# The last stage of a fused audio tower: bias rows without cleared rows, weight rests by another instruction form, and probabilities that travel with the tokens

## The chip, the cores and the metric

The kernel runs on one core of a Trainium2 chip. The metric is the device time of that core in microseconds (us). The median of three runs before the change is 1778.48 us (1774.12 to 1779.3).

## What is computed

The reference is a two-layer tower over 4 batches of 750 tokens of 192 numbers each: a token mixer, a linear-attention block with a causal part, a gated mixture of 8 experts with the best two taken, a window attention with relative positions, and last a mixture of 8 experts with the best one taken. Only the last is changed by intent:

```
xt = _layernorm(h).reshape(-1, 192)            # 3000 tokens
logits = xt @ Ws + bs;  probs = softmax(logits)
routes = argmax(probs);  prob_max = max(probs)
hid = gelu(xt @ W1[route] + b1[route])         # 192 -> 768
y = hid @ W2[route] + b2[route]                # 768 -> 192
out = h + y * prob_max
```

Everything is float32.

## The kernel before, in words

One program holds the four stages one behind the other; the function `moe` (L789 on) is run twice, once gated (name `m0`, the second stage) and once not (name `m1`, the last stage). In `m1`, token row t of a batch lies on partition p, with 125 partitions and 24 tiles, so the whole `h` is a tile of 125 x 24 x 192.

**Front part of the last stage.** The five engines run from instruction lists of their own and wait on semaphores. DVE takes the statistics and normalises (L1314), TensorE turns the tiles (L1068) and makes the logits (L1079), ACT brings them out (L1236, L1241) and takes the exponential (L1260). DVE finds each token's expert (L1394 to L1410), TensorE counts (L1101, L1102), and DVE works out a slot for every token: 31 groups ("tiles") of 128 slots, each with one expert. The list of tokens per slot comes from a product of two one-hot tables (`lane1` L1451, then L1111) and is turned into indices `take` and `give` (L1461 to L1476). `lane1` shares its memory with the normalised tokens, so DVE waits (`s_X`) until these have been stored.

**The rows X.** SP stores h and the normalised tokens side by side in DRAM as a row of 2 x 192 numbers per token (L940). A tensor of 125 partitions is stored in two parts, partitions 0 to 111 and 112 to 124. GpSimd gathers 128 rows by `take` (L1006) when all of X is stored (`s_X`) and `take` is there.

**Weights in two parts.** For accuracy each product is made of three: weights and tokens are split into a rounded value and its rest. ACT makes the rounded weights (`round_weights`, L1225 to L1227, three instructions an expert), DVE the rests (`rest_of_weights`, L1309 and L1310, a subtraction of two tensors each). `w1[:, e, 3, :]` holds the rest of rows 128 to 191 in partitions 0 to 63 and, in partitions 64 and 96, the bias in two parts; GpSimd clears partitions 64 to 127 of it first (L998, eight instructions), and the tokens' side `xB` has ones there. SP puts the two bias rows in place (L957).

**Order before the loop.** ACT rounds experts 0 to 2 between its logits work and 3 to 7 behind the exponential. DVE makes the rests 0 to 2 early, and 3 to 7 behind `take`; then it makes the probabilities (L1481 to L1484), splits them in three bf16 parts and spreads them into a table `tileP` (L1492 to L1496). TensorE waits for all weights, turns the first two gathered groups (L1118, L1119), with ACT (L1272 to L1275) and DVE (L1506, L1507, L1510) splitting them, makes the first group's first products (L1129) and then 24 products of `lane1` and `tileP` (L1138) that put each slot's probability in PSUM, from which DVE adds up `prob` (L1556, L1558).

**The loop.** For each group TensorE turns the next but one group, turns the hidden values (L1176), makes the next group's first products (L1129) and this group's second products (L1190). DVE copies (L1523), adds the bias (L1539) and multiplies by the probability and adds the residual `hres` (L1543), a copy of the gathered h (L1510). GpSimd scatters to the output and gathers the group four further on.

Of the kernel before, what the change touches and what calls it, by code (L numbers as in the profile page):

```python
# [12 lines left out]
F32 = mybir.dt.float32  # L13
# [9 lines left out]
E = len(KS) * D  # L23
# [718 lines left out]
PARTS = 3  # L742

FIRST = ((0, 0), (0, 1), (1, 0), (2, 2), (2, 3))
BHI, BLO = 64, 96
# [6 lines left out]
class Moe:  # L752
# [3 lines left out]
    def __init__(self, name, top, width, gated):  # L756
# [9 lines left out]
        self.wide = E if gated else 2 * E  # L766
# [14 lines left out]
def moe(nc, keep, A, h, ident, cfg, out, st=None, w1=None, wr=None, row=None, room=None, share=None, Y=None,  # L781
# [4 lines left out]
    with ctx:  # L786
# [14 lines left out]
        with ExitStack() as late:  # L801
# [3 lines left out]
            hres = None if cfg.gated else late.enter_context(nc.sbuf_tensor(f"{name}_hres", [SLOT, RING, E], F32))  # L805
# [56 lines left out]
        part = None if cfg.gated else sb("part", [P, PARTS, NT], BF16)  # L862
        prob = None if cfg.gated else sb("prob", [128, S])
# [18 lines left out]

        with ExitStack() as early:
            tileP = None if cfg.gated else early.enter_context(
                nc.sbuf_tensor(f"{name}_tileP", [P, NT, PARTS, S], BF16))
# [33 lines left out]
        s_wb, s_wh, s_wl = (None if cfg.gated else sem(k) for k in ("wb", "wh", "wl"))  # L919
# [4 lines left out]
        s_part, s_prob, s_b2, s_hr = (None if cfg.gated else sem(k) for k in ("part", "prob", "b2", "hr"))  # L924
        stored = 16 * len(ROW_PARTS) * B * (1 if cfg.gated else 2)
# [3 lines left out]
        def _(sp):  # L929
# [21 lines left out]
            if not cfg.gated:  # L951
                sp.dma_start(b2[:].rearrange("p x e -> p (x e)"), A[f"{name}_b2"].partition_broadcast(128)
                             ).then_inc(s_w, 16)
                sp.wait_ge(s_z, 3)
# [11 lines left out]
        def _(pool):  # L966
# [27 lines left out]
            if not cfg.gated:  # L994
                pool.memset(xB[64:128].bitcast(F32), 1.0)
            if not cfg.gated:
                for e in range(NE):
                    last = pool.memset(w1[64:128, e, 3, :].bitcast(F32), 0.0)  # L998
                last.then_inc(s_z, 1)
                pool.wait_ge(s_z, 3)  # L1000
# [56 lines left out]
        def _(pe):  # L1057
# [77 lines left out]
            def probabilities():  # L1135
                pe.wait_ge(s_part, 1)
                for t in range(NT):
                    last = nc.tensor.matmul(psY[:, 256:256 + PARTS * S], lane1[:, 0, t, :],  # L1138
                                            tileP[:, t, :, :].rearrange("p n s -> p (n s)"),
                                            start=(t == 0), stop=(t == NT - 1))  # L1140
                last.then_inc(s_prob, 1)
# [11 lines left out]
            pe.wait_ge(s_xc, 2)  # L1153

# [6 lines left out]
            if not cfg.gated:  # L1161
                probabilities()
# [37 lines left out]
        def _(act):  # L1200
# [102 lines left out]
        def _(dve):  # L1303
# [3 lines left out]
            def rest_of_weights(e):  # L1307
                dve.wait_ge(s_wh, e + 1)
                v.tensor_tensor(w1[:, e, 1, :], w1[:, e, 1, :].bitcast(F32), w1[:, e, 0, :].bitcast(F32), ALU.subtract)  # L1309
                v.tensor_tensor(w1[0:64, e, 3, :], w1[0:64, e, 3, :].bitcast(F32), w1[0:64, e, 2, :].bitcast(F32),  # L1310
                                ALU.subtract).then_inc(s_wl, 1)
# [97 lines left out]
            else:  # L1409
                v.tensor_copy(msk[:], oh[:, 0]).then_inc(s_m, 1)  # L1410

# [69 lines left out]
            link(v.tensor_reduce(lm[:], lg[:], AX.X, ALU.add))  # L1481
            link(v.reciprocal(lm[:], lm[:]))
            for k in range(top):
                link(v.tensor_tensor(pe_[:, k, :], pe_[:, k, :], lm[:], ALU.mult))  # L1484
# [1325 lines left out]
```

## Time and profile before

| | |
|---|---|
| median of three runs | 1778.48 us |
| the profiled execution | 1779.27 us |
| its span | 1777.5 us |
| TensorE matmul busy | 1545.6 us, 87% |
| VectorE (DVE) busy | 1198.3 us, 67% |
| ScalarE (ACT) busy | 990.7 us, 56% |
| GpSimd (POOL) busy | 343.4 us, 19% |
| DMA packets, bytes | 61940, 94.86 MB |

The last stage starts at 1547.5 us of the span and the loop's first product at 1621.3 us. Shares over the whole span are of little use here, since the change touches some 75 us; the stage has to be read in order of time.

### The profile page before, as it was taken

How to read it: one execution, taken by the hardware profiler on the slowest of the kernel's cores; microseconds unless marked ns; L12 is line 12 of the kernel's file. 1: busy time of each engine (PE TensorE's matmuls, PEld its weight loads, DVE VectorE, ACT ScalarE, POOL GpSimd, SP SyncE). 2: the span in 40 equal slices, each digit the busy share in tenths (PEclk: the TensorE clock that was granted, in tenths of full speed). 3: DMA queues.
4: the chain of work that ended last, by engine and by line, in shares of the span. 5: the costliest groups of instructions: out<-in, count | busy, mean ns of one | idle time of the engine just before them, and what ended most of it. 6: DMA issues, size and time to landing. Idle time of an engine off the chain costs nothing. (4 is left out here: it accounts for less than half of the span.)

```text
span 1777.5 us, 32284 instructions
## 1 busy us (share of the span) xinstructions
PE 1545.6 (87%) x10815; PEld 1432.0 (81%) x10816; DVE 1198.3 (67%) x2259; ACT 990.7 (56%) x1818; POOL 343.4 (19%) x507
## 2 busy tenths in 40 slices
PE   4873899945999999899999899899999999646997
PEld 4762899944899899898899899799999889526996
DVE  3878555547785786785787686687777587485553
ACT  6433222224777578577577678577668657262221
POOL 4130566650100110110010010010010000103443
PEclk6886899976998999999899999999999899757999
DMA  8203111145101101100110110110110100191121
GB/s 257 68 23 95 45 56 57 58 118 141 43 11 37 43 11 37 45 11 18 29 43 10 30 44 19 28 43 19 29 43 19 28 8 19 45 311 46 59 61 30
DMA packets 61940, 94.86 MB, mean 53 GB/s; under 512 B 15645, under 2 KB 46512, under 8 KB 61423
## 3 DMA queue, kind: packets, MB, share of 16 engines
q1 hardware_dynamic: 52606, 72.92, 13.9%
q0 software_dynamic: 9200, 20.21, 3.9%
q8 instruction: 78, 1.28, 0.3%
q14 instruction: 56, 0.45, 0.1%
HBM read 72.58 MB, written 21.06 MB: 53 GB/s over the span
## 5 line engine op out<-in xcount | busy, mean ns | idle before, releaser
L2690 DVE TENSOR_TENSOR a_Plo<-a_PT,a_Phi 125x756 fp32r<-125x756 f32 x288 | 281.9, 979 | 72.5 <-ACT a_PT L2415 71.5
L2415 ACT ACTIVATE a_Phi<-a_S 125x756 fp32r<-125x756 f32 x288 | 231.2, 803 | 152.0 <-PE a_O L2209 128.4
L2580 DVE TENSOR_REDUCE a_nmx<-a_M 125x1 f32<-125x752 f32 x248 | 232.7, 938 | 102.9 <-PE a_M L2084 101.9
L1904 POOL TENSOR_TENSOR a_qlo<-a_work,a_qhi 127x750 fp32r<-127x750 f32 x48 | 79.2, 1659 | 1012.6 <-PE a_S L2190 510.9
L2415 ACT ACTIVATE a_PT<-a_S 125x756 f32<-125x756 f32 x288 | 230.3, 800 | 0.0
L1129 PE MATMUL m_psG<-m_w,m_xT 128*128 x788 | 167.3, 351 | 5.1 <-issue 2.3
L2190 PE MATMUL a_S<-a_qhi,a_khi 128*125 128x378 f32 x576 | 153.5, 348 | 10.0 <-DVE a_nmx L2580 6.8
L2202 PE MATMUL a_O<-a_Phi,a_vhi 125*128 125x378 f32 x576 | 150.3, 342 | 1.4 <-issue 1.1
L2209 PE MATMUL a_O<-a_Plo,a_vhi 125*128 125x378 f32 x576 | 147.5, 337 | 0.4 <-DVE a_Plo L2690 0.2
L2190 PE MATMUL a_S<-a_qhi,a_klo 128*125 128x378 f32 x576 | 147.6, 338 | 0.0
L2190 PE MATMUL a_S<-a_qlo,a_khi 128*125 128x378 f32 x576 | 147.0, 336 | 0.0
L2205 PE MATMUL a_O<-a_Phi,a_vlo 125*64 125x378 f32 x576 | 146.4, 336 | 0.0
L1129 PEld LDWEIGHTS m_psG<-m_w,m_xT 128*128 128x128 f32 x788 | 136.6, 191 | 12.1 <-issue 10.4
L1190 PE MATMUL m_psY<-m_w,m_hidT 128*128 x696 | 130.0, 330 | 2.6 <-DVE m_hidT L1523 2.6
L2084 PE MATMUL a_M<-a_khi,a_qhi 127*125 127x376 f32 x496 | 128.4, 340 | 0.4 <-DVE a_nmx L2580 0.4
L1190 PEld LDWEIGHTS m_psY<-m_w,m_hidT 128*128 128x128 f32 x696 | 114.3, 189 | 9.4 <-issue 9.4
L2209 PEld LDWEIGHTS a_O<-a_Plo,a_vhi 125*128 125x128 f32 x576 | 104.1, 189 | 13.9 <-DVE a_Plo L2690 3.7
L2190 PEld LDWEIGHTS a_S<-a_qhi,a_khi 128*125 128x125 f32 x576 | 100.2, 188 | 16.9 <-issue 10.5
L1272 ACT ACTIVATE m_xT<-m_psX 128x128 fp32r<-128x128 f32 x85 | 23.6, 277 | 159.9 <-PE m_psX L1119 83.5
L2202 PEld LDWEIGHTS a_O<-a_Phi,a_vhi 125*128 125x128 f32 x576 | 102.1, 190 | 10.7 <-issue 9.3
L2190 PEld LDWEIGHTS a_S<-a_qhi,a_klo 128*125 128x125 f32 x576 | 104.2, 187 | 0.0
L2190 PEld LDWEIGHTS a_S<-a_qlo,a_khi 128*125 128x125 f32 x576 | 104.0, 187 | 0.0
(431 smaller groups left out, 3017.1 us busy)
## 6 DMA issues: line engine op xcount, KB each, us to landing
a_qhi<-a_rdens SPq DMA_DIRECT2D x48, 187.5 KB, 3.3
m_w<-in_m_w SPq DMA_DIRECT2D x16, 384.0 KB, 7.2
a_wkv<-a_w4k SPq DMA_DIRECT2D x8, 768.0 KB, 4.9
a_wq<-a_w4q SPq DMA_DIRECT2D x8, 768.0 KB, 6.3
a_wkv<-a_w4v SPq DMA_DIRECT2D x8, 768.0 KB, 5.9
m_w<-in_m_w SPq DMA_DIRECT2D x8, 576.0 KB
m_X<-m_xn SPq DMA_DIRECT2D x8, 504.0 KB
m_w<-in_m_w SPq DMA_DIRECT2D x16, 192.0 KB, 7.5
```

The costliest lines, as they stand in the source:

```text
L1129: last = nc.tensor.matmul(psG[buf][:, g, 0:half], tokens, w1[0:rows_, bass.ds(e, 1), k, g * half:(g + 1) * half].rearrange("d o f -> d (o ...
L1190: last = nc.tensor.matmul(psY[:, 0:E], hidT[:, k * 128:(k + 1) * 128], w2[:, bass.ds(here, 1), k, :].rearrange("f o e -> f (o e)"), start= ...
L1272: nc.scalar.activation(xT[:, buf, 0, :], psX[:, 0:SLOT], ACT.Copy)
L1904: pool.tensor_tensor(qlo[0:ONE, u % HG % QLO, :], work[0:ONE, u % HG, 0:L], qhi[0:ONE, u % HG, :].bitcast(F32), ALU.subtract).then_inc(sg[ ...
L2084: last = nc.tensor.matmul(bank[0:P, a, 0:376], qhi[0:ONE, u % HG, c * P:(c + 1) * P], khi[0:ONE, u % HG, a * 374:a * 374 + 376], start=Tru ...
L2190: last = nc.tensor.matmul(psS[wd % 2][0:P, a, 0:HP], kk[:, u % HG, at], qq[:, PART[a]:PART[a] + HP], start=(x == 0), stop=(x == 2))
L2202: nc.tensor.matmul(psO[:, a, 0:HP], vhi[:, c, u % HG, :], Phi[:, wd % 2, at[a]], start=(c == 0), stop=False)
L2205: nc.tensor.matmul(psO[0:HD, a, 0:HP], vlo[:, c, u % HG, :], Phi[:, wd % 2, at[a]], start=False, stop=False)
L2209: last = nc.tensor.matmul(psO[:, a, 0:HP], vhi[:, c, u % HG, :], Plo[:, wd % 2, at[a]], start=False, stop=(c == CH - 1))
L2415: last = nc.scalar.activation(to[:, wd % 2, :].rearrange("p (a l) -> p a l", a=2), psS[wd % 2][0:P, :, 0:HP], ACT.Exp, scale=SCALE)
L2580: v.tensor_reduce(nmx[:, u % 2, c:c + 1], bank[0:P, :, 0:376], AX.XY, ALU.max, negate=True).then_inc(sg["max_ready"], 1)
L2690: v.tensor_tensor(Plo[:, wd % 2, :], PT[:, wd % 2, :], Phi[:, wd % 2, :].bitcast(F32), ALU.subtract).then_inc(sg["exp_rest"], 1)
```

## The change

In the last stage only:

- The rows of X get one number more (385 instead of 384). ACT stores each token's probability behind its row, one DMA with 3000 elements of 4 bytes, each in its own row; `s_X` counts it too. The gathered group then holds its probabilities as column 384, `hres` copies 193 columns, and L1543's successor reads the probability from there. The bf16 parts, `tileP`, the 24 products and the sums in PSUM go.
- DVE makes the probabilities right behind the expert's mask, and the rest of expert 3 behind them, while it waits for the counts; ACT rounds expert 3 before the exponential and experts 4 to 7 behind the store.
- The bias rows lie in partitions 64 and 65, so nothing has to be cleared (the eight GpSimd instructions go), and the product over these rows takes 66 rows instead of 97.
- The rests are written as one instruction with three operands, (w x 1.0) - rounded.
- TensorE turns the first two groups before it waits for the weights (in both `moe` stages), and DVE splits the first group before the rest of expert 7.

```diff
-BHI, BLO = 64, 96
+BHI, BLO = 64, 65
...
-        self.wide = E if gated else 2 * E
+        self.wide = E if gated else 2 * E + 1
...
+        stored = 16 * (len(ROW_PARTS) * B * (1 if cfg.gated else 2) + (not cfg.gated))
...
-                for e in range(NE):
-                    last = pool.memset(w1[64:128, e, 3, :].bitcast(F32), 0.0)
...
-            pe.wait_ge(s_eid, 1)
-            pe.wait_ge(s_w, 16 * (NE + (0 if cfg.gated else 3)))
-            if not cfg.gated:
-                pe.wait_ge(s_wl, NE)
-                pe.wait_ge(s_z, 3)
             for j in range(2):
                 pe.wait_ge(s_in[j], 16)
                 if j:
                     pe.wait_ge(s_xc, 1)
                 to_columns(j)
             pe.wait_ge(s_xc, 2)
+            pe.wait_ge(s_eid, 1)
+            pe.wait_ge(s_w, 16 * (NE + (0 if cfg.gated else 3)))
+            if not cfg.gated:
+                pe.wait_ge(s_wl, NE)
+                pe.wait_ge(s_xo, 1)
...
-            if not cfg.gated:
-                probabilities()
...
+            if not cfg.gated:
+                round_weights(soon)
             act.wait_ge(s_ls, 1)
             nc.scalar.activation(lg[:], lg[:], ACT.Exp).then_inc(s_ex, 1)
...
-                for e in range(soon, NE):
+                act.wait_ge(s_prob, 1)
+                act.dma_start(X[:, 2 * E:].rearrange("(t p) o -> p (t o)", p=P), pe_[:, 0, :],
+                              allow_slow_non_contiguous=True).then_inc(s_X, 16)
+                for e in range(soon + 1, NE):
                     round_weights(e)
...
-                v.tensor_tensor(w1[:, e, 1, :], w1[:, e, 1, :].bitcast(F32), w1[:, e, 0, :].bitcast(F32), ALU.subtract)
+                v.scalar_tensor_tensor(w1[:, e, 1, :], w1[:, e, 1, :].bitcast(F32), 1.0, w1[:, e, 0, :].bitcast(F32),
+                                       ALU.mult, ALU.subtract)
...
                 v.tensor_copy(msk[:], oh[:, 0]).then_inc(s_m, 1)
+                link(v.tensor_reduce(lm[:], lg[:], AX.X, ALU.add))
+                link(v.reciprocal(lm[:], lm[:]))
+                v.tensor_tensor(pe_[:, 0, :], pe_[:, 0, :], lm[:], ALU.mult).then_inc(s_prob, 1)
+                rest_of_weights(3)
...
-                for e in range(3, NE):
+                for e in range(4, NE):
+                    if e == NE - 1:
+                        rest_of_tokens(0, 0)
                     rest_of_weights(e)
+                rest_of_tokens(0, 1)
...
-                        v.scalar_tensor_tensor(y[:, j, :], y[:, j, :], prob[:, bass.ds(RING * i + j, 1)],
-                                               hres[:, j, :], ALU.mult, ALU.add).then_inc(s_y, 1)
+                        v.scalar_tensor_tensor(y[:, j, :], y[:, j, :], hres[:, j, E:], hres[:, j, 0:E], ALU.mult,
+                                               ALU.add).then_inc(s_y, 1)
```

## Rows read from the trace of the kernel before

**Rows 1.** The chain that ended last, last stage: start us, us, what.

```profile
1551.63 4.74 DVE m_xn L1314 x6
1591.18 3.28 DVE m_lane L1451
1598.20 0.86 DVE m_w L1309
...
1611.93 0.45 PE m_psX L1118
...
1614.67 3.56 PE m_psG L1129 x10
1618.24 1.91 PE m_psY L1138 x24
...
1620.60 0.73 PE m_psH L1176 x6
1621.33 1.74 PE m_psG L1129 x10
```

**Rows 2.** Timeline of DVE: start us, us, engine, line, operation, [idle before].

```profile
1558.68 1.83 DVE L1314 TENSOR_SCALAR m_xn<-h,m_mv,m_rstd 125x192 f32<-125x192 f32 x6
1582.87 0.36 DVE L1414 COPY m_tot<-m_psG 128x192 f32<-128x192 f32 x1 [1.74 <-PE m_psG L1102]
1606.80 0.34 DVE L1481 TENSOR_REDUCE m_lm<-m_lg 125x24 f32<-125x192 f32 x1
1607.73 0.18 DVE L1492 CAST m_part<-m_pe 125x24 bf16<-125x24 f32 x1
```

**Rows 3.** Timeline of ACT.

```profile
1576.01 0.28 ACT L1241 ACTIVATE m_lgT<-m_psX 128x125 f32<-128x125 f32 x1 [1.22 <-PE m_psX L1079]
1578.31 0.36 ACT L1260 ACTIVATE m_lg<-m_lg 125x192 f32<-125x192 f32 x1 [2.03 <-DVE m_lg L1387]
1580.10 0.82 ACT L1225 ACTIVATE m_w<-m_w 128x768 fp32r<-128x768 f32 x1
...
1582.54 0.83 ACT L1225 ACTIVATE m_w<-m_w 128x768 fp32r<-128x768 f32 x1
```

**Rows 4.** Timeline of POOL.

```profile
1550.21 6.05 POOL L998 MEMSET m_w<- 64x768 f32 x8
1599.02 1.82 POOL L1006 DMA_INDIRECT m_xg<-m_X,m_take  x1 [40.18 <-DVE m_take L1476]
```

**Rows 5.** DVE groups by shape, whole span: busy us, mean ns | idle before.

```profile
L1539 DVE TENSOR_TENSOR m_y<-m_psY,m_b 128x192 f32<-128x192 f32 x31 | 11.1, 358 | 69.0 <-PE m_psY L1190 55.9 <-issue 13.0
L1396 DVE SCALAR_TENSOR_TENSOR m_tmp<-m_tmp,m_iotx 125x192 f32<-125x192 f32 x3 | 1.1, 357 | 0.1
L1400 DVE TENSOR_TENSOR m_oh<-m_iotx,m_idx 125x192 f32<-125x192 f32 x3 | 1.1, 357 | 0.1
```

**Rows 6.** DMA, 1588 to 1596 us, 40 slices: GB/s.

```profile
GB/s 507 461 392 415 392 392 392 507 479 369 415 369 392 392 484 438 415 415 392 369 392 438 422 522 430 353 422 430 430 399 430 445 307 231 62 31 0 0 46 31
```

**Rows 7.** DMA, 1604 to 1612 us: GB/s by slices of 0.2 us (the gathers).

```profile
GB/s 207 161 92 323 184 15 0 0 0 230 138 292 261 62 0 0 0 92 138 184 361 192 16 0 0 0 0 0 0 0 0 0 0 0 0 0 0 0 0 0
```

**Rows 8.** DMA queues, 1562 to 1563 us: packets, MB, share of 16 engines.

```profile
q1 hardware_dynamic: 90, 0.21, 56.1%
q0 software_dynamic: 90, 0.19, 52.3%
```

**Rows 9.** DMA busy tenths by 0.0125 us, 539.1 to 539.6 us: a store of 150 pieces of 40 bytes from 75 partitions.

```profile
DMA  0000000001333337656465420000000000001000
```

**Rows 10.** DMA, 1548.8 to 1549.2 us: a load of 32 bytes into each of 125 partitions.

```profile
DMA packets 38, 0.00 MB, mean 3 GB/s; under 512 B 38, under 2 KB 38, under 8 KB 38
```

**Rows 11.** A window with loads of 125 rows: us, engines' busy time, clock, DMA share, GB/s.

```profile
388.25:388.50 0.25, 0.00 (x0) 0.00 (x0) 0.25 (x2) 0.00 (x0) 0.25 (x2) 0.50 0.21 55
```

**Rows 12.** DMA queue, 1584 to 1592 us (second weights): packets, MB, share.

```profile
q1 hardware_dynamic: 818, 3.33, 101.8%
```

**Rows 13.** Timeline of SP: the stores of h.

```profile
1557.62 12.36 SPq L940 DMA_DIRECT2D m_X<-h  x8
```

More of the change, by code:

```diff
@@ L804, in moe @@
             y = late.enter_context(nc.sbuf_tensor(f"{name}_y", [SLOT, RING, E], F32))
-            hres = None if cfg.gated else late.enter_context(nc.sbuf_tensor(f"{name}_hres", [SLOT, RING, E], F32))
+            hres = None if cfg.gated else late.enter_context(nc.sbuf_tensor(f"{name}_hres", [SLOT, RING, E + 1], F32))
         xn = sb("xn", [P, NT, E])
@@ L881, in moe @@
         hid = sb("hid", [SLOT, cfg.width])
-        with ExitStack() as early:
-            tileP = None if cfg.gated else early.enter_context(
-                nc.sbuf_tensor(f"{name}_tileP", [P, NT, PARTS, S], BF16))
         hidT = sb("hidT", [128, cfg.width])
@@ L918, in moe @@
         s_w1 = [] if cfg.gated else [sem(f"w1_{e}") for e in range(NE)]
-        s_wb, s_wh, s_wl = (None if cfg.gated else sem(k) for k in ("wb", "wh", "wl"))
+        s_wb, s_wh, s_wl, s_xo = (None if cfg.gated else sem(k) for k in ("wb", "wh", "wl", "xo"))
         s_xh = sem("xh")
@@ L922, in moe @@
             "xt", "xc", "gu", "sg", "h", "ht", "hc", "c", "y"))
-        s_part, s_prob, s_b2, s_hr = (None if cfg.gated else sem(k) for k in ("part", "prob", "b2", "hr"))
-        stored = 16 * len(ROW_PARTS) * B * (1 if cfg.gated else 2)
+        s_prob, s_b2, s_hr = (None if cfg.gated else sem(k) for k in ("prob", "b2", "hr"))
+        stored = 16 * (len(ROW_PARTS) * B * (1 if cfg.gated else 2) + (not cfg.gated))
         block = ctx.enter_context(nc.Block())
@@ L994, in _ @@
             if not cfg.gated:
[L995 to L1000 removed]
+                pool.memset(xB[64:128].bitcast(F32), 1.0).then_inc(s_xo, 1)
+                pool.wait_ge(s_xo, 1)
             for j in range(RING):
@@ L1133, in first_products @@
                     last.then_inc(s_gu, 1)
[L1135 to L1141, printed above, removed]
-            pe.wait_ge(s_eid, 1)
-            pe.wait_ge(s_w, 16 * (NE + (0 if cfg.gated else 3)))
-            if not cfg.gated:
-                pe.wait_ge(s_wl, NE)
-                pe.wait_ge(s_z, 3)
             for j in range(2):
@@ L1478, in _ @@
             if not cfg.gated:
-                for e in range(3, NE):
+                for e in range(4, NE):
+                    if e == NE - 1:
+                        rest_of_tokens(0, 0)
                     rest_of_weights(e)
[L1481 to L1484, printed above, removed]
+                rest_of_tokens(0, 1)
             if cfg.gated:
+                link(v.tensor_reduce(lm[:], lg[:], AX.X, ALU.add))
+                link(v.reciprocal(lm[:], lm[:]))
+                for k in range(top):
+                    link(v.tensor_tensor(pe_[:, k, :], pe_[:, k, :], lm[:], ALU.mult))
                 for b in range(B):
@@ L1488, in _ @@
                     v.tensor_tensor(h[:, at_, :], h[:, at_, :], n[:, at_, :], ALU.add)
-            if not cfg.gated:
-                for x in range(PARTS):
-                    link(v.tensor_copy(part[:, x, :], pe_[:, 0, :] if x == 0 else lm[:]))
-                    if x + 1 < PARTS:
-                        link(v.tensor_tensor(lm[:], pe_[:, 0, :] if x == 0 else lm[:], part[:, x, :], ALU.subtract))
-                dve.wait_ge(s_w, 16 * (NE + 3))
-                v.tensor_tensor(tileP[:], tile0[:, 0].unsqueeze(2).broadcast_to([P, NT, PARTS, S]),
-                                part[:].rearrange("p x t -> p t x").unsqueeze(3).broadcast_to([P, NT, PARTS, S]),
-                                ALU.mult).then_inc(s_part, 1)
             v.sem_inc(s_h, 1)
@@ L1554, in _ @@
                 dve.wait_ge(s_eid, 1)
-                dve.wait_ge(s_prob, 1)
-                link(v.tensor_copy(prob[:], psY[:, 256:256 + S]))
-                for x in range(1, PARTS):
-                    link(v.tensor_tensor(prob[:], prob[:], psY[:, 256 + x * S:256 + (x + 1) * S], ALU.add))
             hidden_columns(0, 0)
```

28 lines of the change are left out of this document (12 added, 16 removed).

## The prediction

> **What bounds the kernel now.** Over the span TensorE leads, but the change lies in one stage, so I read that stage's chain of waits first, then the timelines of DVE, ACT and POOL beside it, and last the DMA in short windows, because the change adds a DMA that two engines wait for. The chain [rows 1] shows where an edit can move the end. It runs through the first six normalisations (4.74 us), ACT's logits work, DVE's slot arithmetic, `lane1` from 1591.1, and `take` at 1598.2; then only DVE: ten weight rests until 1606.9, the probabilities and `tileP`, the split of the first two groups, and at 1614.67 TensorE's first products (3.56 us). Then come 24 probability products (1.91 us), and the loop, bound by TensorE. In it DVE waits 69 us for the second products before L1539 [rows 5], and the change leaves TensorE's loop work as it is, so the whole effect is by how much the point "first products" and what follows up to the loop moves.
>
> **The parts.** All is set against the profiled execution: 1779.27 us, span 1777.5, some 1.8 us around it; it is 0.8 us above the median of the runs.
>
> (a) Clearing gone. POOL's eight instructions ran from 1550.2 to 1556.3 [rows 4]. In this time six normalisations took 4.74 us; the next six took 1.83 [rows 1, 2]. So DVE was held up by 2.9 us on the path. Behind it ACT works nearly without a gap and its first expert's rounding comes in between; I take 2.0 us of the 2.9 (bounds 0 and 2.9) as reaching the exponential.
>
> (b) ACT rounds expert 3 before the exponential: 2.44 us (1582.54 - 1580.10), from 1576.2 on, ends at 1578.6 where the exponential started at 1578.31 [rows 3]: +0.3 us.
>
> (c) DVE gets the probabilities (0.93 us, 1606.80 to 1607.73) and one rest (2 x 0.87 = 1.74 us, the step from one to the next [rows 1]) into a wait of 1.74 us [rows 2]: 2.67 - 1.74 = +0.93 us before `lane1`.
>
> So if nothing else holds it, `lane1` can start at 1591.1 - 2.0 + 0.3 + 0.9 = 1590.3.
>
> (d) From `lane1` to the first products. `take` is done 7.1 us after the start of `lane1` [rows 1]. Of the second gather the data landed by about 1605.1 [rows 7], allow 0.3 for the signal: 7.2 us behind `take`. Turn, rounding, rest of the second group up to the first products took 1614.67 - 1611.93 = 2.74 us [rows 1]. Sum 7.1 + 7.2 + 2.8 = 17.1 us, against 23.6 before (1591.1 to 1614.67). DVE's own work in it is 6 x 0.87 + 0.9 + 1.74 = 7.9 us, ready before the second group's 7.2 + 0.7 + 0.6 = 8.5; it is hidden. Moving TensorE's turns ahead of its wait for the weights costs nothing: before, it stood idle there. In the gated stage the same move changes nothing, since its weights are there long before the gather (a gain is bounded by 0 there; a loss would need something ready later than the gather, and TensorE has nothing queued but these turns).
>
> (e) Three-operand form. No row shows it on 768 columns. On 192 columns and with a constant it takes 357 ns, the two-operand form as well [rows 5], so I take the step of 0.87 us again: 0. The bound is what the first gather's issue costs beside these instructions: 1.82 us [rows 4] where in the loop it is about 1.0; a form that left GpSimd alone would give up to 0.8 us, one that hindered it more as much again.
>
> (f) 24 products gone: from the end of the first products the next turns began after 1.91 us. Now TensorE has to wait there for the activation, which the products had hidden: by estimate the 1620.6 - 1618.2 = 2.4 us shrink to 1.1, -1.3. But the first ten of L1129 took 3.56 us and the next ten 1.74 [rows 1]: TensorE's pace doubled while these products ran. With a gap in their place the six turns of L1176, at least, come at the slow pace (0.73 us more), and if the second ten do too it is 1.8 more. I take -0.6, bounds -1.3 and +1.2.
>
> (g) 193 columns instead of 192, one pointer operand from another place: DVE waits in each turn [rows 5]; 0. The stores of X get a row step of 1540 bytes; no row shows such a step: between 0 and, by the 16 us that the stores take, 10% of them; I take 0 and keep 1.6 us for the upper end.
>
> Without (h) this is 1590.3 + 17.1 - 1614.67 - 0.6 = -7.9 us.
>
> (h) The new store. It has 3000 pieces of 4 bytes from 125 partitions, is issued about 1581 (the mask's end less what (a) gives, plus 0.9 for (c) and 0.3 for (b)), and `lane1`, on DVE with all the rests queued behind it, waits for it; so does GpSimd's gather. What does it take alone? Lower bound: a store of 150 pieces of 40 bytes from 75 partitions moved in 16 slices of 0.0125 us, 0.20 us, 750 a us: 3000 / 750 = 4.0 us [rows 9]. Upper bound: the load of 32 bytes to each of 125 partitions brought 38 packets in 0.4 us, 95 a us: 31.6 us [rows 10]. What differs is how many DMA engines work: other loads of 125 rows kept 0.21 of the 16 busy [rows 11], where the store of 75 partitions reached 0.7 [rows 9]. I take a third of the lower bound's rate, 250 a us: 12 us.
>
> It isn't alone. The DMA engines are full until about 1594.8 [rows 6], with packets of the second weights, 818 in 8 us: 6.4 per engine and us [rows 12]. Where two queues had work, each got as many packets as the other: 90 and 90 [rows 8]. So the small pieces pass at the pace of the large ones: from 1581.5 to 1594.8 some 80 to 85 per engine. If a third of the engines carry 600 each, that is 13%; the rest, 87% of 12 us = 10.4, comes afterwards, with 0.7 for what the interleaving itself delays and 0.5 for the last to land: 1606.4. `lane1` starts then instead of at 1590.3, and the total is 1606.4 + 17.1 - 1614.67 - 0.6 = +8.2 us. With the lower bound (all engines, 188 each, 43% passed): 1594.8 + 0.6 x 4 + 1.0 = 1598.2, that is 0.0. With the upper: 1594.8 + 27.5 + 1.2 = 1623.5, +25.3.
>
> ACT's issue may be held until most pieces are out (SP's was, by 12.4 us for eight, at the stores of h [rows 13]), and behind it stand experts 4 to 7 (9.8 us). Held until 1603, ACT is done at 1613; DVE needs expert 4 at 1613.5 (`take`) and 7 at 1619: hidden, with 2 us to spare or more.
>
> By the Trainium skill, "DMA: Bandwidth & Descriptors", section "Why a DMA increments its semaphore by 16 and not by 1", a DMA uses the largest number of engines up to 16 that divides the slowest dimension. For 125 that would be 5, so 600 pieces each; the share of [rows 11] agrees as far as it goes (0.21 of 16 is 3.4 engines), and the kernel stores its rows as 112 and 13. By the same page's "Rules for kernel authors" each strided element is a descriptor of its own, which gives the 3000. Were all 16 engines used, the sum would be the one of the lower bound.
>
> **The rivals.**
>
> Rival 1, no wait: the store lands before 1590.3. Then it is 1771.4 us. For it: it has 9 us, and alone it would need 4 at the lower bound; it holds if its pieces don't take turns with the weights one for one. Against it: [rows 8] and the full engines.
>
> Rival 2, a short wait: more engines, or pieces at their own pace (1581.5 + 12 + 0.5 = 1594), so `lane1` at 1594 to 1600 and -4.2 to +1.8 us: about 1778. For it: the store of [rows 9]. Against: the 125 partitions.
>
> Rival 3, the long one: one piece each 10.5 ns as in [rows 10], 1623.5, so +25.3: 1804.6. For it: this is the only transfer with 125 partitions and such small pieces; against: it was a load, with a DRAM read in each piece.
>
> **How the numbers follow.** Forecast 0.38, rival 1 0.27, rival 2 0.22, rival 3 0.13. The predicted time is 1779.27 + 8.2 = 1787.5, its own range 1783 to 1794. The range for all has to reach down to rival 1 (1771.4, less 0.9 for the bounds of (a) and (e)) and up towards rival 3, short of its end: 1770.5 to 1800. About 0.3%, 5.3 us, is what a measurement of this kernel can tell from no change. Faster by more: rival 1 and a little of rival 2, 0.29. Same: most of rival 2 and the lower edge of the forecast, 0.23. Slower: 0.48.
>
> **What would show it.** The first six normalisations at 1.8 us confirm (a). DVE's idle time before `lane1`, ended by a DMA, is (h): 16 us by the forecast, 0 by rival 1, 4 to 10 by rival 2, 33 by rival 3. The DMA share in the window behind the weights should be near 0.1 to 0.3 with thousands of packets under 512 bytes. From `lane1` to the first products it should be 17 us, and first products to the first L1176 about 4.6. The rests should be 940 ns each. I'm wrong if `lane1` starts without a wait, or if the issue on ACT holds up the rounding so long that DVE waits for it.

## The result, and the profile of the changed kernel

The changed kernel takes 1786.23 us (median of five runs, 1782.19 to 1790.52), the one before 1778.45 us beside it (five runs, 1774.12 to 1779.3). The ratio is 1.0063, with a 95% interval of 1.0043 to 1.0082: slower by 11.2 us (7.6 to 14.6); the two medians of five, taken alone, lie 7.8 us apart. Forecast were 1787.5 us and +8.2 us, both within the interval. The profiled execution of the changed kernel is the lowest of its five, 1782.19 us with a span of 1780.4, so the two profiled spans alone differ by only 2.9 us. The last stage is therefore compared by its own clock: from GpSimd's first instruction in it (1547.50 us before, 1539.14 after) to the end of the program. This start lies 8.4 us apart. Ahead of it only two turns of TensorE were moved (in the gated stage), and the starts in the twelve traces of this study scatter from 1538.2 to 1551.1 us, with and without that move in no order, so I take it for scatter. The last stage took 230.0 us before and 241.3 after. The difference, +11.3 us, agrees with the ratio.

The chain that ended last, in the changed kernel (start us, us, what), answers to [rows 1]:

```profile
1571.67 30.26 DMA m_X<-m_pe
1601.95 3.37 DVE m_lane L1449
...
1609.88 4.00 DMA m_xg<-m_X,m_take
...
1619.21 3.58 PE m_psG L1118 x10
1622.89 0.82 ACT m_hid L1275
1623.84 1.54 PE m_psH L1155 x6
1625.38 3.20 PE m_psG L1118 x10
1628.58 2.10 PE m_psY L1169 x12
```

The first line is new: a DMA of 12 KB, the store of the probabilities, holds the chain for 30.26 us. The timeline of DVE in the changed kernel (start us, us, engine, line, operation, in brackets the idle time before it and what ended it) answers to [rows 2]:

```profile
1543.27 1.93 DVE L1308 TENSOR_SCALAR m_xn<-h,m_mv,m_rstd 125x192 f32<-125x192 f32 x6
...
1580.66 0.93 DVE L1445 TENSOR_TENSOR m_tile<-m_tile,m_num_t 125x744 bf16<-125x744 bf16 x1
1601.95 3.36 DVE L1449 TENSOR_TENSOR m_lane<-m_iotl,m_lane 125x3072 bf16<-125x3072 bf16 x1 [20.36 <-DMA m_X<-m_pe]
...
1678.01 0.36 DVE L1521 TENSOR_TENSOR m_y<-m_psY,m_b 128x192 f32<-128x192 f32 x1 [2.14 <-PE m_psY L1169]
1678.40 0.42 DVE L1525 SCALAR_TENSOR_TENSOR m_y<-m_y,m_hres 128x192 f32<-128x192 f32 x1
```

The first six normalisations take 1.93 us instead of 4.74. DVE, ready for `lane1` at 1581.6, stands for 20.36 us until the store has landed. The timeline of ACT in the changed kernel answers to [rows 3]; ACTq is its DMA queue's own row:

```profile
1571.67 0.54 ACTq L1245 DMA_DIRECT2D m_X<-m_pe  x1
1572.26 0.84 ACT L1204 ACTIVATE m_w<-m_w 128x768 fp32r<-128x768 f32 x1 [2.38 <-DVE m_pe L1407]
```

The issue took 0.54 us and held up nothing on ACT. So the 30 us are the transfer and what it waits for.

Table of the stage for every kernel that ran, us from the stage's start; the points are read from each kernel's timelines. "FP" is the first group's first products, "Y" the first second-products; the last three columns are differences.

```
kernel               exp  lane1    FP      Y    end | wait before lane1 | lane1 to FP | FP to Y | Y to end
before             30.81  43.59  67.17  75.40  230.0 |   0    | 23.58 | 8.23 | 154.6
after              28.87  62.81  80.07  89.24  241.3 | 20.36  | 17.26 | 9.17 | 152.0
e1_sixteen         28.90  61.88  79.11  86.20  238.1 | 19.42  | 17.23 | 7.09 | 151.9
e2_no_store        28.87  42.36  59.57  66.50  218.4 |   0    | 17.21 | 6.93 | 151.9
e4_spread_kept     28.89  42.38  59.69  66.63  221.2 |   0    | 17.31 | 6.94 | 154.6
e9_only_later      28.87  46.61  68.06  76.81  228.7 |  4.17  | 21.45 | 8.75 | 151.9
e6_bias_rows       28.56  41.34  64.91  72.47  227.1 |   0    | 23.57 | 7.56 | 154.6
e7_three_operands  30.71  43.49  67.16  75.29  229.9 |   0    | 23.67 | 8.13 | 154.6
e10_fixed_column   28.88  42.35  59.95  68.14  220.0 |   0    | 17.60 | 8.19 | 151.9
e11_column_copied  28.89  42.36  59.59  66.69  219.5 |   0    | 17.23 | 7.10 | 152.8
e8_own_tensor      28.79  54.55  73.40  82.56  242.5 | 12.18  | 18.85 | 9.16 | 159.9
e5_sixteen_later   28.87  46.32  67.89  76.74  228.6 |  3.88  | 21.57 | 8.85 | 151.9
```

From before to after: `lane1` +19.2 (a wait of 20.4, less 1.2), `lane1` to first products -6.3, from there to the second products +0.9, the rest -2.6. The sum is 11.2.

### The profile page after: what moved, and what is told of

The parts are those of the page before. It is cut to its first block and busy times, and to the rows that moved or that the text cites. A ratio compares the mean times of both kernels' runs of the same rounds, so it can differ in the third digit from the quotient of the medians.

```text
span 1780.4 us, 32189 instructions
## 1 busy us (share of the span) xinstructions
PE 1542.1 (87%) x10791; PEld 1434.0 (81%) x10792; DVE 1191.9 (67%) x2250; ACT 990.3 (56%) x1818; POOL 337.4 (19%) x499
## 3 DMA queue, kind: packets, MB, share of 16 engines
q10 hardware_dynamic: 3005, 0.01, 0.2%
## 5 line engine op out<-in xcount | busy, mean ns | idle before, releaser
L2169 PEld LDWEIGHTS a_S<-a_qhi,a_khi 128*125 128x125 f32 x576 | 99.6, 187 | 17.2 <-issue 10.3
```

The lines of the kernel that those rows point to most:

```text
L2169: last = nc.tensor.matmul(psS[wd % 2][0:P, a, 0:HP], kk[:, u % HG, at], qq[:, PART[a]:PART[a] + HP], start=(x == 0), stop=(x == 2))
```

## The experiments

The theory: the store of the probabilities costs all of the loss and more, its few DMA engines and the turns that it takes with the weights being the cause, and the other parts of the change gain. Rivals: the store is slow only because it uses few engines; another part (a rule of TensorE's clock, ACT's issue) costs; or the gain comes from the products' going and so can't be had without the store.

### e2_no_store: the changed kernel without the store

The rows stay at 384 columns, and the probability is left out: the rows are multiplied by 1.

```diff
-                act.wait_ge(s_prob, 1)
-                act.dma_start(X[:, 2 * E:].rearrange("(t p) o -> p (t o)", p=P), pe_[:, 0, :], ...)
...
-                        v.scalar_tensor_tensor(y[:, j, :], y[:, j, :], hres[:, j, E:], hres[:, j, 0:E], ...
+                        v.scalar_tensor_tensor(y[:, j, :], y[:, j, :], ones[:, 0:1], hres[:, j, 0:E], ...
```

> The changed kernel without the store of the probabilities, with rows of 384 numbers again; the probability is left out of the result (the residual is added to the unscaled product). Theory 1: no wait before the one-hot table at all, the table starts about 42.4 us behind the stage's start (1581.5 - 1539.1), the stage is 241.3 - 20.4 = 221 us, and the time 8 to 10 us under that of the kernel before. The stores of the rows go back to 36.7 ns a packet. Rival B (something else makes the stage longer): the stage stays above 228. Theory 2, on the clock (TensorE's first products of the second group run at the low level, 3.2 us instead of 1.74, because nothing fills the gap that the 24 products left): still so here, since it doesn't hang on the store.

Measured: 1762.76 us (7 runs) against 1773.85, ratio 0.9939 [0.9915, 0.9962]. No wait before `lane1`, which starts 42.36 us into the stage, as theory 1 had it. Theory 2, that the second group's first products stay at the low clock, didn't come true here: the stretch from the first products to the second takes 6.93 us instead of 9.17 (more under (f) below). DVE's timeline:

```profile
1593.47 3.35 DVE L1446 TENSOR_TENSOR m_lane<-m_iotl,m_lane 125x3072 bf16<-125x3072 bf16 x1
```

The stage is 22.9 us shorter than after's. The store and the wider row behind it cost 20.4 of these in the wait; 2.2 more lie between the first products and the second (below).

### e1_sixteen: the same store in two parts, of 112 and 13 partitions

```diff
-                act.dma_start(X[:, 2 * E:].rearrange("(t p) o -> p (t o)", p=P), pe_[:, 0, :], ...).then_inc(s_X, 16)
+                for ps in ROW_PARTS:
+                    act.dma_start(X[:, 2 * E:2 * E + 1].rearrange("(t p) o -> p (t o)", p=P)[ps], pe_[ps, 0, :],
+                                  ...).then_inc(s_X, 16)
```

> The changed kernel, only its store of the probabilities is made in two parts, partitions 0 to 111 and 112 to 124, as the other stores of rows are. 'Stage' is the time from GpSimd's first instruction of the last stage to the end of the span: 230.0 us before the change (1777.5 - 1547.5), 241.3 after it (1780.4 - 1539.1). Theory 1 (the wait for the store of 3000 pieces on few DMA engines, taking turns with the weights): 188 pieces per engine instead of 600, nearly all passed while the second weights run, so DVE's wait before the one-hot table shrinks from 20.4 us to 13 to 15 and the stage to 234 to 236. Rival A (the pieces are slow as such, each a write of 4 bytes, however they are spread): the wait stays at 18 us or more and the stage above 239. Rival B (the stage is longer for its wider rows and other things, not for the store): the stage stays at 241.

Measured: 1783.14 us (10 runs), ratio 1.0053 [1.0029, 1.0076]. The wait hardly moved, a miss for theory 1, and the stage of 238.1 us lies between it (234 to 236) and the rivals (239 or more): 0.9 us of the 3.2 are won in the wait, 2.1 between the first products and the second, where the clock differs (below). The timelines of DVE and of ACT's queue:

```profile
1570.78 15.42 ACTq L1246 DMA_DIRECT2D m_X<-m_pe  x2
...
1600.11 3.36 DVE L1450 TENSOR_TENSOR m_lane<-m_iotl,m_lane 125x3072 bf16<-125x3072 bf16 x1 [19.42 <-DMA m_X<-m_xn]
```

The reading of it is in the queues (packets, MB, share of the 16 DMA engines). Of the changed kernel: the whole page; 1575 to 1577 us, in which rows of X are still stored; 1584 to 1592, in which the second weights move; 1595 to 1597, where they end; 1596 to 1598.

```profile
q10 hardware_dynamic: 3005, 0.01, 0.2%
...
q1 hardware_dynamic: 369, 0.29, 116.1%
q10 hardware_dynamic: 1, 0.00, 0.0%
...
q1 hardware_dynamic: 783, 3.25, 99.5%
q10 hardware_dynamic: 249, 0.00, 1.8%
...
q10 hardware_dynamic: 993, 0.00, 46.0%
q1 hardware_dynamic: 23, 0.04, 5.4%
...
q10 hardware_dynamic: 1088, 0.00, 55.2%
```

3005 packets are 3000 pieces and 5 others: the store ran on five engines. The Trainium skill, "DMA: Bandwidth & Descriptors", section "Why a DMA increments its semaphore by 16 and not by 1", gives the largest number up to 16 that divides the slowest dimension, which for 125 is 5, and one completion on each; the trace agrees with its 3005. Issued at 1571.67, the store had moved one packet by 1577. Beside the weights, queue 1 moved 783 packets on 16 engines, so 245 on five of them if they are spread evenly, and queue 10 moved 249: one for one. When the weights ended, at about 1595.5, some 2,000 pieces were left; 1088 of them went in 2 us over five engines, one per 9.2 ns and engine, and the last about 1600.1. `lane1` started 1.8 us after that (1.6 in e8, 1.8 in e9), so the landing is a part of the wait too.

The same view of e1, of 1575 to 1577 and of 1597 to 1599 us:

```profile
q10 hardware_dynamic: 756, 0.00, 95.4%
q1 hardware_dynamic: 239, 0.17, 68.9%
...
q10 hardware_dynamic: 184, 0.00, 5.2%
q1 hardware_dynamic: 54, 0.18, 28.1%
```

The tail is gone, as expected: the last pieces land with the last weights. But the weights end 60 us into e1's stage and 56 into after's. In e1 the pieces run on all engines beside the row stores, and are dear there: the time of 756 of them adds up to 95% of 16 engines for 2 us, 40 ns each, against 16 ns each in the changed kernel's tail (55.2% for 1088). The shares of two queues overlap (95 and 69 are more than 100), so 40 ns is what a piece was under way, not what it took from its engine; but queue 1 moved only 239 packets in these 2 us (369 in after). More engines save the tail of 5 us and delay what all engines had to move by nearly as much. The two issues together took ACT 15.42 us, where the single one took 0.54.

### e9_only_later: the second weights wait until all rows are stored

```diff
+            if not cfg.gated:
+                sp.wait_ge(s_X, stored)
             for e in range(NE):
                 sp.dma_start(w2[:, e], A[f"{name}_w2"][:, e]).then_inc(s_w, 16)
```

> The changed kernel, only SP waits for all stores of the rows, the probabilities among them, before it issues the second weights. Theory 1 (1:1 turns with the weights make the store late): without them the pieces take turns only with the rest of the row stores and then go at 9 ns each per engine, so the wait for the store falls from 20.4 us to about 4, the table starts 46 to 47 us behind the stage's start, and the second weights (13.5 us) and bias rows land just before TensorE needs them: stage 225 to 227. Rival A (pieces slow as such, whatever runs beside them): the wait stays above 12 us, stage above 233. Rival D (the postponed weights become the bound): the table starts early, but the first products wait for a DMA, stage 228 to 232.

Measured: 1772.13 us (10 runs), ratio 0.9989 [0.9961, 1.0018]. The timelines of DVE, POOL and PE:

```profile
1594.31 3.36 DVE L1451 TENSOR_TENSOR m_lane<-m_iotl,m_lane 125x3072 bf16<-125x3072 bf16 x1 [4.17 <-DMA m_X<-m_pe]
1602.24 1.83 POOL L997 DMA_INDIRECT m_xg<-m_X,m_take  x1 [49.19 <-DVE m_take L1476]
1610.10 0.47 PE L1109 MATMUL m_psX<-ident,m_xg 128*128 128x128 f32 x1 [10.89 <-DMA m_xg<-m_X,m_take]
```

The store alone, on its five engines, leaves a wait of 4.17 us instead of 20.36, so most of the wait is what moves beside the store, not its own length. But the weights now move beside the gathers. From the gather's issue to the first turn it is 7.9 us (1602.24 to 1610.10); in the changed kernel it was 4.0 (its rows, of the same timelines):

```profile
1609.88 1.83 POOL L995 DMA_INDIRECT m_xg<-m_X,m_take  x1 [65.39 <-DVE m_take L1474]
1613.92 0.47 PE L1107 MATMUL m_psX<-ident,m_xg 128*128 128x128 f32 x1 [7.07 <-DMA m_xg<-m_X,m_take]
```

`lane1` to first products is 21.45 us instead of 17.26. Of the 16 us gained, 4 are given back. The wait and the start of `lane1` came as theory 1 had them; the stage, 228.7 us, did not (225 to 227) and lies where rival D had it.

### e5_sixteen_later: both edits

> The changed kernel with both: the store in two parts (16 and 13 engines) and the second weights issued only when all rows are stored. Theory 1: the 188 pieces per engine pass beside the row stores, which end 45 us behind the stage's start in e1_sixteen, and nothing trails: table at 45 to 46 us (46.6 with the weights postponed alone, 61.9 with the store in two parts alone). The gathers then run beside the weights as in e9_only_later, where the first group's turn came 7.9 us after its gather's issue instead of 4.0: first products 21 to 21.5 us behind the table instead of 17.3, stage 226 to 229. Rival A: the wait stays above 10 us (table at 52 or later).

Measured: one run, 1780.04 us beside 1774.46 (its stage began at 1549.66, late among these kernels); the stage took 228.6 us, as e9's 228.7. The wait is 3.88 instead of 4.17. With the weights out of the way, sixteen engines win 0.3 us, by one trace of each.

### e8_own_tensor: the probabilities in a tensor of their own

The rows of X have 384 columns again (a step of 1536 bytes), the 3000 pieces lie side by side in DRAM, and a second gather per group brings them.

```diff
-        self.wide = E if gated else 2 * E + 1
+        self.wide = E if gated else 2 * E
+        XP = ... nc.dram_tensor(f"{name}_XP", (NTOK, 1), F32, kind="Internal").ap()
...
-                act.dma_start(X[:, 2 * E:].rearrange("(t p) o -> p (t o)", p=P), pe_[:, 0, :], ...
+                act.dma_start(XP.rearrange("(t p) o -> p (t o)", p=P), pe_[:, 0, :], ...
...
+                    pool.indirect_dma_start(out=xg[:, j, cfg.wide:], out_offset=None, in_=XP, ...
```

> The changed kernel, but the probabilities go to a DRAM tensor of their own (3000 x 1, still 3000 pieces of 4 bytes from 125 partitions, one DMA) and are gathered by a second, 4-byte gather for each group; the rows of X are 384 numbers wide again. Theory 4 (the wait of 20.4 us has two parts: the row step of 1540 bytes makes the row stores 28% slower, and the pieces take turns with the weights and trail them): row stores at 360 GB/s again in the window 20 to 28 us behind the stage's start (260 in the changed kernel, 361 in the one without a store), the weights end at 49 to 50 us instead of 56, some 480 pieces per engine are left then at 10 ns, and the table starts at 55 to 57 us instead of 62.8. Rival F (the row step costs nothing that counts, the store alone makes the wait): table at 61 us or later. Total and loop are not what this run is for, as GpSimd issues twice as many gathers.

Measured: one run, 1785.92 us beside 1774.46; the stage is 242.5 us, since the second gather lengthens the loop to 159.9. The use of the run is the wait, 12.18 us instead of 20.36:

```profile
1596.27 3.36 DVE L1455 TENSOR_TENSOR m_lane<-m_iotl,m_lane 125x3072 bf16<-125x3072 bf16 x1 [12.18 <-DMA m_XP<-m_pe]
```

In queue 1 the weights end at about 1590, 48 us into its stage, as in e2 (47) and not as in after (56):

```profile
q10 hardware_dynamic: 854, 0.00, 38.5%
q1 hardware_dynamic: 36, 0.07, 9.1%
```

These are the queues of e8 from 1589 to 1591 us. The 8.2 us that the wait lost are therefore put down to the row step of 1540 bytes, which delays the weights and with them the store. That the pieces lie side by side in DRAM is in the same run; little is left for it, since the weights alone end 8 us earlier and the tails are alike: from the end of the weights to the last piece it is 4.9 us for some 2,300 pieces in e8 and 4.7 for some 2,000 in the changed kernel. The DMA line of 8 us, 20 to 28 us into the stage, of the changed kernel, of e2 and of e8:

```profile
DMA packets 2728, 2.08 MB, mean 260 GB/s; under 512 B 101, under 2 KB 2706, under 8 KB 2727
```

```profile
DMA packets 3880, 2.89 MB, mean 361 GB/s; under 512 B 140, under 2 KB 3878, under 8 KB 3879
```

```profile
DMA packets 3898, 2.90 MB, mean 362 GB/s; under 512 B 144, under 2 KB 3897, under 8 KB 3897
```

The same 768-byte pieces move at 260 GB/s with the odd step and at 361 without it. The other traces agree: in their 8 us it is 251 to 272 GB/s in the four kernels with the step of 1540 bytes (after, e1, e5, e9) and 339 to 364 in the eight with 1536, with a store of probabilities (e8) and without one. SP's issues of the second eight stores are held longer in the changed kernel (first fence) than in e2 (second), and the weights stand behind them:

```profile
1563.13 10.14 SPq L934 DMA_DIRECT2D m_X<-m_xn  x8
```

```profile
1574.10 8.19 SPq L934 DMA_DIRECT2D m_X<-m_xn  x8
```

### e4_spread_kept: every part but the store

The 24 products, `part`, `tileP` and `prob` stay, behind the moved turns and rests.

```diff
-                act.dma_start(X[:, 2 * E:].rearrange("(t p) o -> p (t o)", p=P), pe_[:, 0, :], ...
...
             first_products(0, ...)
+            if not cfg.gated:
+                probabilities()
...
-                        v.scalar_tensor_tensor(y[:, j, :], y[:, j, :], hres[:, j, E:], hres[:, j, 0:E], ...
+                        v.scalar_tensor_tensor(y[:, j, :], y[:, j, :], prob[:, bass.ds(RING * i + j, 1)], hres[:, j, :], ...
```

> The changed kernel, but the probabilities go to their slots by the 24 products as before the change, with rows of 384 numbers and no store; DVE makes the table for them behind the second group's split, beside TensorE's first products. All else of the change is in it, and the result is complete. Theory 1: no wait, as in the kernel without the store; from the first products to the second products' start it takes 8.4 us as before the change instead of 9.2, since the 24 products fill the gap and the next ten come at the high clock: stage 220 to 222 us, time 8 to 10 us under the kernel before (1769 to 1771), 16 to 20 under the changed one. Rival C (the gain of the change's other parts is small or is hidden behind the gathers): stage 226 to 230.

Measured: 1766.53 us (10 runs), ratio 0.9959 [0.9939, 0.998]. Up to the second products it stands within 0.2 us of e2, which has no products at all (66.63 and 66.50). PE's timeline:

```profile
1610.37 1.23 PE L1134 MATMUL m_psY<-m_tileP,m_lane 125*128 125x93 bf16 x24
```

In 1.23 us, behind the first products, they fill the time in which TensorE waits for the activation. At this clock, what the store was to save costs nothing before the loop. The forecast of 8.4 us from the first products to the second was missed, on the good side (6.94), since the clock rose earlier than it had before the change.

### e10_fixed_column and e11_column_copied: the pointer operand

The loop from the second products to the end takes 154.6 us in before, e4, e6 and e7, and 152.0 in after, e1, e2 and e9. What parts them is the operand `prob[:, bass.ds(RING * i + j, 1)]`, a column whose address stands in a register. e10 is e4 with a fixed column (all turns of the loop then take the first columns' probabilities); e11 copies the column beside the row's copy, where DVE has time, and the late instruction has a fixed address.

```diff
-    v.scalar_tensor_tensor(y[:, j, :], y[:, j, :], prob[:, bass.ds(RING * i + j, 1)], hres[:, j, :], ...
+    v.scalar_tensor_tensor(y[:, j, :], y[:, j, :], prob[:, j:j + 1], hres[:, j, :], ...        # e10
...
+    v.tensor_copy(hres[:, j % RING, E:], prob[:, bass.ds(RING * i + j, 1)])                    # e11
...
+    v.scalar_tensor_tensor(y[:, j, :], y[:, j, :], hres[:, j, E:], hres[:, j, 0:E], ...        # e11
```

> The kernel with the probabilities spread by products and all other parts of the change (e4_spread_kept), but DVE's last instruction of each group reads the probability from a column whose place doesn't depend on the loop's register (columns 0 to 3 in turn), so wrong probabilities are applied from the fifth group on. Theory 3 (the loop is 2.6 us shorter in the changed kernel because a register sum before this instruction, 0.09 us between L1539's start and L1543's, is gone from the path that frees PSUM for TensorE): from the first second products to the span's end 151.9 us as in the changed kernel and the one without a store, not 154.6 as in e4_spread_kept and 154.4 before the change. Rival E (the loop is shorter for 66 rows in place of 97, or for where the tiles lie): it stays at 154.6, since e4_spread_kept has the 66 rows too and this kernel its tiles.

> e4_spread_kept with the probability of each group copied behind its residual (one instruction of one column, addressed by the loop's register, beside the split of the group two further on, where DVE waits for TensorE anyway), so that the last instruction reads it from a fixed place as in the changed kernel. The result is complete. Theory 3: the loop part 151.9 to 152.2 us, stage 218.5 to 219 against 221.2 of e4_spread_kept and 241.3 of the changed kernel; total 0.5 to 0.6% under the kernel before (0.9941 to 0.995 of it). If the new instruction is not hidden: loop part 154 or more and a ratio like e4's, 0.996.

Measured: e10, one run, 1762.7 us, and the loop is 151.9: the operand is the whole of the 2.6 us. e11 is the best kernel of this study with a complete result, 1763.2 us (6 runs) against 1775.03, ratio 0.9935 [0.9911, 0.996], a little under the forecast 0.9941 to 0.995. Its loop takes 152.8 and its stage 219.5, each some 0.5 us over what was forecast: the new copy is hidden for the most part, not wholly. The timelines of DVE, of before and of e11:

```profile
1673.46 0.36 DVE L1539 TENSOR_TENSOR m_y<-m_psY,m_b 128x192 f32<-128x192 f32 x1 [2.15 <-PE m_psY L1190]
1673.94 0.42 DVE L1543 SCALAR_TENSOR_TENSOR m_y<-m_y,m_prob,m_hres 128x192 f32<-128x192 f32 x1
```

```profile
1666.84 0.15 DVE L1320 COPY m_hres<-m_prob 128x1 f32 x1
...
1669.25 0.36 DVE L1546 TENSOR_TENSOR m_y<-m_psY,m_b 128x192 f32<-128x192 f32 x1 [2.08 <-PE m_psY L1186]
1669.64 0.42 DVE L1550 SCALAR_TENSOR_TENSOR m_y<-m_y,m_hres 128x192 f32<-128x192 f32 x1
```

Both instructions last the same; from the start of the first to the start of the second it is 0.48 us before and 0.39 in e11. Of the 31 turns [rows 5], 28 show the 0.09 us; the last three stand at 0.39 before the change too. 28 x 0.09 = 2.5 us, near the 2.6 measured. The way to TensorE can be seen as well. The next instruction on DVE is the copy that makes `hidT`, and TensorE loads `hidT` as the weights of the second products. The page's groups of these loads, before and in the changed kernel:

```profile
L1190 PEld LDWEIGHTS m_psY<-m_w,m_hidT 128*128 128x128 f32 x696 | 114.3, 189 | 9.4 <-issue 9.4
L1169 PEld LDWEIGHTS m_psY<-m_w,m_hidT 128*128 128x128 f32 x696 | 114.6, 190 | 6.9 <-issue 4.8
```

The idle time ahead of them is 9.4 to 9.6 us in the four kernels with the register's operand in this place, 6.8 to 6.9 in after, e1, e2, e5, e9 and e10, and 7.8 in e11: the differences are those of the loops (154.6, 151.9, 152.8).

### e6_bias_rows and e7_three_operands: two parts alone, in the kernel before

e6 puts the bias rows at 64 and 65 and clears nothing; e7 writes the rests with three operands.

```diff
-BHI, BLO = 64, 96
+BHI, BLO = 64, 65
...
-                for e in range(NE):
-                    last = pool.memset(w1[64:128, e, 3, :].bitcast(F32), 0.0)
```

```diff
-    v.tensor_tensor(w1[:, e, 1, :], w1[:, e, 1, :].bitcast(F32), w1[:, e, 0, :].bitcast(F32), ALU.subtract)
+    v.scalar_tensor_tensor(w1[:, e, 1, :], w1[:, e, 1, :].bitcast(F32), 1.0, w1[:, e, 0, :].bitcast(F32),
+                           ALU.mult, ALU.subtract)
```

> The kernel before the change with the bias rows in partitions 64 and 65 and without the eight clearing instructions, nothing else. Theory: the first six normalisations take 1.83 us instead of 4.74, and of the 2.9 us some 2.0 to 2.3 arrive at the exponential (30.8 us behind the stage's start before the change), so the exponential at 28.5 to 28.8 and the stage at 227.7 to 228 us (230.0 before). Rival: ACT, which follows, takes it all: the exponential stays at 30.5 or later, stage 230. 66 rows in place of 97 cost TensorE the same: turns in the loop as before.

> The kernel before the change with the rests of the weights as one instruction with three operands and the constant 1, nothing else. Theory: 0.94 us each with steps of 0.87, the gather's issue beside them 1.8 us as before, stage 229.5 to 230.5, the same time. Rival: the form works in another way on GpSimd's gather: the issues take 1.0 us and the stage is 0.8 us shorter, or they take 2.6 and it is longer by as much.

Measured: e6 1768.85 us (10 runs), ratio 0.9965 [0.9944, 0.9985]; e7 1775.7 us (10 runs), ratio 1.0011 [0.9989, 1.0034]. The timelines of DVE and ACT in e6, and of POOL in e7:

```profile
1548.77 1.92 DVE L1310 TENSOR_SCALAR m_xn<-h,m_mv,m_rstd 125x192 f32<-125x192 f32 x6
1573.20 0.36 ACT L1256 ACTIVATE m_lg<-m_lg 125x192 f32<-125x192 f32 x1 [2.03 <-DVE m_lg L1383]
```

```profile
1590.73 1.83 POOL L1006 DMA_INDIRECT m_xg<-m_X,m_take  x1 [40.08 <-DVE m_take L1477]
```

In e6 the exponential starts 28.56 us into the stage instead of 30.81: of the 2.8 us that the clearing took from DVE, 2.25 reach it. The stage is 2.9 us shorter; the 0.7 beyond the 2.25 lie between the first products and the second (7.56 us instead of 8.23), where the clock rose earlier. The loop stays at 154.6, so 66 rows in place of 97 cost TensorE the same. In e7 the gather's issue takes 1.83 us as in [rows 4], and the stage is 229.9 against 230.0: the form of the rests is worth nothing.

## Why the prediction was right, point by point

The sign, the sum (+8.2 us forecast, +11.2 measured) and the place were right. That the sum came so near is in part luck, as (h) shows. The terms:

- **(a), (b), (c), `lane1` without the wait.** Forecast -2.0 + 0.3 + 0.9 = -0.8; e2 shows 42.36 - 43.59 = -1.2. The clearing gives 2.25 (e6), the earlier rounding costs 0.3 (28.87 against 28.56), the probabilities and one rest cost 0.7.
- **(d), `lane1` to first products.** Forecast 17.1 us, measured 17.26, and 17.2 to 17.3 in e1, e2, e4 and e11 (17.6 in e10). The number was right, one part of its account wasn't: DVE's own work was to be hidden behind the second gather, with 0.6 us to spare. In the changed kernel ACT had split the second group by 1617.31, and DVE, on the rest of expert 7 until then, took it up only at 1617.81. No kernel has the moved turns and rests alone; the 6.3 us are theirs by the chain.
- **(e), the three-operand form.** 0, as e7 shows.
- **(f), the 24 products.** Forecast -0.6, measured +0.9, within the bounds. By e2 and e4 the products are worth 0.0. But the stretch from first to second products takes 6.9 to 9.2 us in kernels with one and the same stream there, and the granted clock differs with it. Windows (us, then busy us and count of PE, PEld, DVE, ACT, POOL, the granted clock as a share of 2.4 GHz, DMA share, GB/s) of the changed kernel, then of e1, e2 and before:

```profile
1623.80:1628.30 4.50, 4.46 (x16) 4.47 (x17) 1.70 (x4) 0.39 (x3) 0.00 (x0) 0.50 0.00 0
1628.40:1633.00 4.60, 4.60 (x31) 4.54 (x29) 1.36 (x3) 1.41 (x4) 0.00 (x0) 0.96 0.01 4
```

```profile
1620.90:1624.40 3.50, 2.86 (x18) 2.44 (x17) 1.44 (x3) 1.29 (x4) 0.00 (x0) 0.93 0.00 0
```

```profile
1614.30:1617.60 3.30, 2.46 (x16) 2.47 (x17) 1.45 (x4) 1.19 (x4) 0.00 (x0) 1.00 0.00 0
```

```profile
1618.20:1620.60 2.40, 2.40 (x28) 2.36 (x27) 0.31 (x2) 0.81 (x1) 0.00 (x0) 0.50 0.00 0
```

The changed kernel was still at 1.2 GHz in its second ten products, where e1, with the same instructions, had risen to 2.4. The table's column "FP to Y" falls into two groups. Where the clock rose within some 4 us of the first products, it is 6.9 to 7.6 us, with the 24 products (e4, e6, e11) and without them (e1, e2). Where it rose later, kernels with the products had it up by the six turns (0.84 to 0.94 us) and took 8.1 to 8.2 us (before, e7, e10), and those without made the turns at 1.2 GHz (1.54 us) and most of the next ten first products too, and took 8.8 to 9.2 (after, e5, e8, e9). That is the slow pace behind a gap that the upper bound of this term was for. So the +0.9 fits the products' going, by one trace of each kernel, and is no fixed cost: in e1 and e2 it isn't there.
- **(g), 193 columns.** The operand "from another place" was taken at 0 because DVE waits in each turn [rows 5]; it gave 2.6 us (e10), within no bound of mine. The step that failed: DVE's idle time was taken as cover, but it lies ahead of the bias and this instruction, and the copy of `hidT`, for which TensorE's weight loads wait, lies behind them. The row step of 1540 bytes was taken at 0 with 1.6 kept for the upper end, as 10% of the stores' 16 us; it costs 8.2 us of the wait, the largest single miss.
- **(h), the store.** Forecast: a wait of 16 us; measured 20.36. The one-for-one turns beside the weights were right (249 against 245), and a third of the engines was right (5 of 16). Alone the store was taken at 12 us; at one piece per 9.2 ns and engine it is 600 x 9.2 = 5.5 us, so this term was too large by about half. The weights, taken to end where they did before, 47 us into the stage, ended at 56. Some 1,000 of the 3000 pieces had passed by then, where 13% were forecast, and from there to `lane1` it was 6.4 us, forecast 11.6. The last piece was given 0.5 us to land, for which no row stood; it was 1.8. So an error of +9 us and one of -5 have opposite signs, and the sum hides them. Without the odd step the wait is 12.2 us (e8), 4 below the forecast. That the issue on ACT is held did not come true with one store; it did with two.

The errors of the terms with their signs: wait +4.4, (f) +1.5, loop -2.6, `lane1` without the wait -0.4, (d) +0.2; together +3.1, which is 11.3 - 8.2.

Of the rivals: no wait and the short wait are excluded by the 20.36 us; the long one by the pieces' own rate, 1088 in 2 us where it had 190. Of the signs named beforehand, the first normalisations (1.93 us), first products to the first turn of `hid` (4.63 us for 4.6) and the rests (0.94 us) came as said; the DMA share behind the weights was higher than said (0.55 from 1596 to 1598, for 0.1 to 0.3), with the pieces in it as said. The sum without (h) was -7.9 us; e2's stage is 11.6 shorter than before's, 7.6 of it up to the first products (forecast 7.3), 1.3 from there to the second products, at another clock, and 2.6 in the loop.

What stays open: why the clock rises at one time and not at another in the same stream, what it is in the step of 1540 bytes that slows the stores, and whether a wider but rounder step would keep the probability in the row and spare the 8.2 us. That wasn't run.

## What to carry to other kernels

A small store with a reader on the critical path can share the engines with whatever else is in their queues, here packet for packet. Count packets per engine, not bytes: the store's 600 on each of five engines were more than the weights had left there, so it ended behind them, however fast it was alone. Look at what a wider row does to all the stores that share it, not only at the one added column. An engine's idle time in a loop is no cover for the instructions behind its wait, if another engine waits for what follows them: there, 0.09 us for an address in a register counted in 28 turns, and copying the operand while the engine waited (e11) took back 1.8 of the 2.6 us.

## What was unexpected of the hardware

- A row step of 1540 bytes lowered the stores of 768-byte pieces from 361 to 260 GB/s.
- Stores of 4 bytes to DRAM went at one per 9.2 ns and engine behind the weights (1088 in 2 us on five engines), 16 ns under way each; beside the row stores they were 40 ns under way each (e1).
- A store issued on one queue while row stores filled another moved one packet in 5 us (1571.67 to 1577).
- From the last piece of the store to the start of the instruction that waited for it, 1.6 to 1.8 us passed (after, e8, e9).
- Two small DMAs issued by ACT held it for 15.42 us (e1; 9.92 in e5); a single one of the same 3000 pieces took 0.54 us.
- An operand addressed by a register put 0.09 us ahead of a DVE instruction whose own length stayed at 0.42 us.
- A gather issued beside a full queue of weights took 7.9 us to the first turn, alone 4.0.
